# Attention with two sets of scores, keys on partitions in the second, in place of transposed probabilities

## The reference

```python
qh = (q @ Wq.T + bq).reshape(B, N_HEADS, Sq, HEAD_DIM)      # 16 heads of 16
kh = (k @ Wk.T + bk).reshape(B, N_HEADS, Skv, HEAD_DIM)
vh = (v @ Wv.T + bv).reshape(B, N_HEADS, Skv, HEAD_DIM)
scores = einsum('bhqd,bhkd->bhqk', qh, kh) / sqrt(HEAD_DIM)
scores = where(causal, -inf, scores)
out = einsum('bhqk,bhkd->bhqd', softmax(scores), vh)
x = x + out.reshape(B, Sq, E) @ Wp.T + bp
x = x + lowprec(gelu(lowprec(layernorm(x), w_fc) + b_fc), w_proj) + b_proj
```

## Time and profile before

| | |
|---|---|
| median of 3 runs | 271.9 us (270.83 to 273.41) |
| span of the profiled execution | 269.2 us |
| attention stage, first mask to the first `ffn_up` | 21.7 to 192.2 us |
| PE busy | 229.3 us |
| DVE busy | 200.8 us |
| ACT busy | 174.9 us |
| POOL busy | 112.7 us |
| mean granted TensorE clock | 0.962 |

### The profile page before, as it was taken

One profiled execution on the slowest core, in us unless ns is written; L12 is line 12 of the kernel. 1 busy time (PEld: TensorE's weight loads), 2 busy tenths in 40 slices (PEclk: granted clock), 3 DMA queues, 4 the chain that ended last, 5 costly groups with the idle time before them and its releaser, 6 DMA issues.

```text
span 269.2 us, 6301 instructions
## 1 busy us (share of the span) xinstructions
PE 229.3 (85%) x2256; PEld 172.3 (64%) x2264; DVE 200.8 (75%) x439; ACT 174.9 (65%) x463; POOL 112.7 (42%) x113
## 2 busy tenths in 40 slices
PE   7877992998999999999999999889749579789963
PEld 7765762776677777777777877667427356456752
DVE  4432473678678979979979776787798999999970
ACT  1344672567967867876876876798835646478962
POOL 2700011003524624633642641441716474569893
PEclk9997997799999999999999999999998979799999
DMA  6681694044334234224225115213031000001111
GB/s 202 170 253 41 198 262 91 2 83 86 69 75 95 71 73 94 72 64 87 49 53 105 43 44 98 61 26 55 2 49 29 19 23 19 33 29 39 42 58 58
DMA packets 37662, 20.35 MB, mean 76 GB/s; under 512 B 12788, under 2 KB 37376, under 8 KB 37632
## 3 DMA queue, kind: packets, MB, share of 16 engines
q1 hardware_dynamic: 34560, 17.14, 27.5%
q10 hardware_dynamic: 3072, 2.82, 3.5%
HBM read 7.35 MB, written 2.10 MB: 35 GB/s over the span
## 4 chain that ended last, share of the span: by engine, by line
PE 48%; DVE 27%; issue 8%; SPq 6%; DMA 5%; POOL 2%; ACT 2%; ACTq 1%; DVEq 0%; POOLq 0%
PE bank L953 13%; PE bank L1015 8%; PE s_banks L1003 7%; DVE hrn L905 7%; DVE h_amax L888 6%; PE s_banks L997 5%; DVE probT L733 5%; PE bank L1057 5%; PE bank L1038 4%; DMA QS<-full 3%; DMA w_rows<-in_L_xattn_Wq 2%; SPq L249 2%; PE bank L929 2%; SPq L242 2%; POOL hq L628 1%
## 5 line engine op out<-in xcount | busy, mean ns | idle before, releaser
L392 ACT ACTIVATE prob<-s_banks,negm 128x128 f32<-128x128 f32 x256 | 72.9, 368 | 38.3 <-DVE negm L725 36.7
L725 DVE TENSOR_REDUCE negm<-s_banks 128x4 f32<-128x512 f32 x64 | 43.8, 686 | 29.4 <-PE s_banks L1003 29.1
L733 DVE COPY probT<-bank 128x512 f32<-128x512 f32 x64 | 43.9, 687 | 10.4 <-PE bank L1015 10.4
L1015 PE MATMUL bank<-ident_f,prob 128*128 128x128 f32 x256 | 41.5, 286 | 7.9 <-DVE probT L733 7.9
L628 POOL TENSOR_TENSOR hq<-hrn,h_mag 128x1024 bf16<-128x1024 f32 x16 | 30.6, 1912 | 24.5 <-DVE hrn L905 24.2
L1015 PEld LDWEIGHTS bank<-ident_f,prob 128*128 128x128 f32 x256 | 28.0, 143 | 16.2 <-issue 12.6
L953 PE MATMUL bank<-cT,wT 128*128 128x256 f32 x128 | 33.2, 406 | 0.0
L525 POOL TENSOR_TENSOR rs<-ve,neg_half 128x2 f32<-128x2 f32 x8 | 6.3, 790 | 56.3 <-DVE ve L678 56.0
L997 PE MATMUL s_banks<-mask_q,ident_b 128*128 128x256 bf16 x128 | 19.9, 280 | 10.0 <-POOL QC L553 5.1
L478 ACT ACTIVATE s_banks<-s_banks 128x512 f32<-128x512 f32 x32 | 18.0, 581 | 15.2 <-PE s_banks L1164 14.6
L953 PEld LDWEIGHTS bank<-cT,wT 128*128 128x128 f32 x128 | 25.1, 206 | 3.2
(11 more groups left out here) (114 smaller groups left out, 409.3 us busy)
## 6 DMA issues: line engine op xcount, KB each, us to landing
oden<-oT SPq DMA_DIRECT2D x64, 64.0 KB, 2.4
KS<-full SPq DMA_DIRECT2D x32, 64.0 KB, 2.3
VS<-full SPq DMA_DIRECT2D x64, 32.0 KB, 2.0
out<-full SPq DMA_DIRECT2D x16, 128.0 KB, 1.7
QS<-full SPq DMA_DIRECT2D x29, 64.0 KB, 2.3
X<-in_x ACTq DMA_DIRECT2D x1, 1536.0 KB, 7.7
cbuf<-in_ctx SPq DMA_DIRECT2D x6, 256.0 KB, 3.0
fc_rows<-in_L_ffn_w_fc SPq DMA_DIRECT2D x1, 1024.0 KB, 5.9
```

Of the source, the lines that this page charges most:

```text
L392: ins = nc.scalar.activation(prob[:, k % 4, u, s, :], s_banks[:, 2 * (k % 2) + u, s * P:(s + 1) * P], ACT.Exp, bias=negm[:, k % 4, u, s:s ...
L725: V.tensor_reduce(negm[:, k % 4, :, :], s_banks[:, 2 * (k % 2):2 * (k % 2) + 2, 0:2 * P].rearrange("p u (s t) -> p u s t", s=2), axis=AX.X ...
L733: V.tensor_copy(probT[:, k % 4, :, :, :].rearrange("p u s t -> p (u s t)"), pt_bank(k)[:, :])\
L1015: ins = T.transpose(pt_bank(k)[:, (2 * u + s) * P:(2 * u + s + 1) * P], prob[:, k % 4, u, s, :], ident_f[:, :])
```

## The change

The scores are computed twice. The first set is as before, queries on partitions, and serves only for the maxima. `turn_maxima` transposes these for two segments at once (16 rows of 128 on TensorE), `copy_maxima` copies them to `negmT` on VectorE, and `move_maxima` moves them by DMA, one for each segment, into row 16 of each group of QC. `keys_apart`, new on ScalarE, copies KS to KX, in which row 16 is 1. The second set has keys on partitions and queries along the columns, with 17 rows: the product then holds score minus maximum. Its exponentials need no bias and are already what `attend` needs, so `transpose_probs`, `copy_pt` and `probT` go. `exps` is two instructions of 128x512.

A `burst` computes both sets: the first for segment s, the second for segment s - 3. Both lie in one bank for each group, with one mask matmul of 512 columns over all four blocks. The mask tile grows from 2 to 4 blocks. Within a burst's banks VectorE and ScalarE take turns: `exps` starts at banks 2 and 3 while `maxes` reads 0 and 1, then they change. The end of the attention stage is written out by hand with bursts that hold one set or both. SyncE's order in a step changes, with the two `move_maxima` in it. QC and KX have three buffers. On GpSimd `power2` stands ahead of `normalise`.

```diff
+NS = NW * NPAIR
...
+LAST = NS - NW
+BURSTS = [(s, s - 3 if s > 2 else None) for s in range(LAST)] + \
+    [(LAST, 25), (None, 26), (29, 27), (30, None), (None, 28), (31, 29), (None, 30), (None, 31)]
+BURST_S = {a: n for n, (a, t) in enumerate(BURSTS) if a is not None}
+BURST_T = {t: n for n, (a, t) in enumerate(BURSTS) if t is not None}
+S_BEFORE = [sum(a is not None for a, t in BURSTS[:n]) for n in range(len(BURSTS) + 1)]
+T_BEFORE = [sum(t is not None for a, t in BURSTS[:n]) for n in range(len(BURSTS) + 1)]
+UNITS = [(2 * u, 2 * u + 1) for u in range(NS // 2 - 1)] + [(30,), (31,)]
...
-        mask_q = sb("mask_q", [P, 2, P], bf16)
+        mask_qt = sb("mask_qt", [P, 4, P], bf16)
...
-        QC = [sb(f"QC{n}", [P, 2 * NM, P]) for n in range(2)]
+        KX = [sb(f"KX{n}", [P, 2 * NM, P]) for n in range(3)]
+        QC = [sb(f"QC{n}", [P, 2 * NM, P]) for n in range(3)]
...
+            def move_maxima(u):
+                sp.wait_ge(sm["mt_copied"], u + 1)
+                for h, s in enumerate(UNITS[u]):
+                    i, w = divmod(s, NW)
+                    sp.dma_start(QC[i % 3][HD::32, 2 * w:2 * w + 2, :].rearrange("p n t -> p (n t)"),
+                                 negmT[u % 2][8 * h:8 * h + 8, :])\
+                      .then_inc(sm["m_moved" if u < len(UNITS) - 1 else "ml_moved"], 16)
...
+                if not first:
+                    move_maxima(2 * i - 1)
                 if not last:
-                    if not first:
-                        sp.wait_ge(sm["s_done"], NW * i)
                     stack_rows(i + 1, 1 - par, 0)
-                if not first:
-                    move_out(i - 1)
-                if not last:
                     if not first:
                         sp.wait_ge(sm["q_apart"], i)
                     stack_rows(i + 1, 1 - par, 1)
+                move_maxima(2 * i)
+                if not last:
                     if not first:
                         sp.wait_ge(sm["v_done"], i)
                     stack_values(i + 1, 1 - par)
+                if not first:
+                    move_out(i - 1)
                 if i < NPAIR - 4:
                     load_ctx(i + 2, par)
             for i in range(NPAIR):
                 step(i, i % 2, i == 0, i == NPAIR - 1)
+            move_maxima(15)
+            move_maxima(16)
             move_out(NPAIR - 1)
...
-            def exps(k):
...
+            def exps(t):
+                n = BURST_T[t]
+                act.wait_ge(sm["burst_done"], n + 1)
+                if t > 1:
+                    act.wait_ge(sm["av_done"], t - 1)
+                for h in (1, 0):
+                    if h == 0 and BURSTS[n][0] is not None:
+                        act.wait_ge(sm["max_done"], 2 * S_BEFORE[n] + 1)
+                    nc.scalar.activation(prob[:, (2 * t + h) % 4, :, :, :].rearrange("p u s t -> p u (s t)"),
+                                         s_banks[:, 2 * h:2 * h + 2, 2 * P:4 * P], ACT.Exp)\
+                        .then_inc(sm["exp_done"], 1)
+            def keys_apart(p, par):
+                act.wait_ge(sm["k_stacked"], 16 * NG * (p + 1))
+                if p > 2:
+                    act.wait_ge(sm["burst_done"], BURST_T[NW * (p - 2) - 1] + 1)
+                nc.scalar.copy(KX[p % 3][:, :, :].rearrange("p n (j w) -> p n j w", j=NJ // KC),
+                               KS[par][:, :].rearrange("p (j n w) -> p n j w", j=NJ // KC, n=2 * NM))\
+                    .then_inc(sm["k_apart"], 1)
...
             def step(i, par, first, last):
-                k = 2 * NW * i
+                if last:
+                    return
+                k = NW * i
+                if k > 2:
+                    exps(k - 3)
+                copy_tx(i + 1)
+                copy_proj(i + 1, 0)
+                if i > 1:
+                    invert(i - 2)
+                if k > 2:
+                    exps(k - 2)
+                    copy_out(i - 1, 0)
+                copy_v(i, par)
+                copy_proj(i + 1, 1)
+                if k > 2:
+                    exps(k - 1)
+                copy_proj(i + 1, 2)
                 exps(k)
-                exps(k + 1)
...
                 if not first:
                     copy_out(i - 1, 1)
-
...
                 if ahead(i):
                     copy_tc(i + 2)
-                if not first and not last:
...
+                keys_apart(i + 1, 1 - par)
+            keys_apart(0, 0)
             steps(act, step)
+            exps(25)
+            copy_weights(0)
+            exps(26)
+            copy_weights(1)
+            invert(NPAIR - 3)
+            exps(27)
+            copy_out(NPAIR - 2, 0)
+            copy_v(NPAIR - 1, 1)
+            copy_weights(2)
+            copy_weights(3)
+            exps(28)
+            copy_out(NPAIR - 2, 1)
+            exps(29)
+            copy_tq(0, 0)
+            copy_tq(1, 1)
+            exps(30)
+            copy_out(NPAIR - 1, 0)
+            invert(NPAIR - 2)
+            exps(31)
...
-            def maxes(k):
...
+            def maxes(s):
+                n = BURST_S[s]
+                dve.wait_ge(sm["burst_done"], n + 1)
+                if s > 3:
+                    dve.wait_ge(sm["mt_done"], UNIT_OF[s - 4] + 1)
+                for h in range(2):
+                    if h and BURSTS[n][1] is not None:
+                        dve.wait_ge(sm["exp_done"], 2 * T_BEFORE[n] + 1)
+                    V.tensor_reduce(negm[:, s % NW, 2 * h:2 * h + 2, :],
+                                    s_banks[:, 2 * h:2 * h + 2, 0:2 * P].rearrange("p u (s t) -> p u s t", s=2),
+                                    axis=AX.X, op=ALU.max, negate=True).then_inc(sm["max_done"], 1)
+            def copy_maxima(u):
+                dve.wait_ge(sm["mt_done"], u + 1)
+                if u > 1:
+                    dve.wait_ge(sm["m_moved"], 16 * (UNITS[u - 2][-1] + 1))
+                n = 2 * len(UNITS[u]) * NG
+                V.tensor_copy(negmT[u % 2][0:n, :], t_bank[0:n, 0:P]).then_inc(sm["mt_copied"], 1)
...
+            def burst(n):
+                s, t = BURSTS[n]
+                if s is not None and s % NW == 0:
+                    pe.wait_ge(sm["k_apart"], s // NW + 1)
+                    pe.wait_ge(sm["q_apart"], s // NW + 1)
+                if n:
+                    pe.wait_ge(sm["max_done"], 2 * S_BEFORE[n])
+                    pe.wait_ge(sm["exp_done"], 2 * T_BEFORE[n])
+                if t is not None:
+                    if t < NS - 1:
+                        pe.wait_ge(sm["m_moved"], 16 * (UNITS[UNIT_OF[t]][-1] + 1))
+                    else:
+                        pe.wait_ge(sm["ml_moved"], 16)
+                lo, hi = (0 if s is not None else 2), (4 if t is not None else 2)
                 for g in range(NG):
-                    T.matmul(s_banks[:, g, 0:2 * P], ident_b[:, :], mask_q[:, :, :].rearrange("p s t -> p (s t)"),
...
+                    T.matmul(s_banks[:, g, lo * P:hi * P], ident_b[:, :],
+                             mask_qt[:, lo:hi, :].rearrange("p s t -> p (s t)"), start=True, stop=False)
+                for c, of in enumerate((s, t)):
+                    if of is None:
+                        continue
+                    i, w = divmod(of, NW)
+                    for h in range(2):
+                        for g in range(NG):
+                            rows = slice(32 * g, 32 * g + HD + c)
+                            queries = QC[i % 3][rows, 2 * w + h, :]
+                            keys = KX[i % 3][rows, 2 * w + h, :]
+                            ins = T.matmul(s_banks[:, g, (2 * c + h) * P:(2 * c + h + 1) * P],
+                                           *((keys, queries) if c else (queries, keys)),
+                                           start=False, stop=(h == 1 and (c == 1 or t is None)))
+                ins.then_inc(sm["burst_done"], 1)
+            def turn_maxima(u):
+                pe.wait_ge(sm["max_done"], 2 * UNITS[u][-1] + 2)
+                if u:
+                    pe.wait_ge(sm["mt_copied"], u)
+                n = 2 * len(UNITS[u]) * NG
+                w = UNITS[u][0] % NW
+                T.transpose(t_bank[0:n, 0:P],
+                            negm[:, w:w + len(UNITS[u]), :, :].rearrange("p w g n -> p (w g n)"), ident_f[:, :])\
+                    .then_inc(sm["mt_done"], 1)
...
-            def attend(i, w):
-                pe.wait_ge(sm["pt_copied"], 2 * (NW * i + w) + 2)
+            def attend(t):
+                i, w = divmod(t, NW)
+                pe.wait_ge(sm["exp_done"], 2 * t + 2)
                 if w == 0:
                     pe.wait_ge(sm["v_copied"], i + 1)
-                if w % 2 == 0 and (w or i):
-                    pe.wait_ge(sm["o_copied"], 2 * i + w // 2)
+                if w % 2 == 0 and t:
+                    pe.wait_ge(sm["o_copied"], t // 2)
                 for s in range(2):
                     b, m = divmod(2 * w + s, NM)
                     for g in range(NG):
```

(92 more changed lines are left out.)

148 lines of the change are left out of this document (32 added, 116 removed).

## The result

The median is 331.6 us (329.05 to 336.22, 4 runs) beside 271.4 (269.80 to 273.41) for the kernel before on the same chip, a ratio of 1.218 with a 95% interval of 1.208 to 1.227. That lies inside the range of 303 to 336 and 10.6 above the 321 predicted. The profiled execution has a span of 334.4, against 269.2 before. It lies near the upper end of its runs, so some 5 of the 65 us by which the spans differ are that execution's own.

A forecast was written before the change was run, and what follows sets the result against it. TensorE bounds the kernel before, SyncE's queue the changed one. Start 2.6, six steps 24.7 and tail 11.8 over 269.2 give 308.3; plus 2.7 to the median, 311; plus half of 20 for the clock, 321 us, range 303 to 336.

The forecast's parts named there:

- What bounds, and the arithmetic: Attention stage: TensorE bounds the kernel before; 4.8 us added against 5.0 removed a step, so its own step becomes 20.6.
- the row: Profile row of today's 16 score passes in a burst, 0.65 us, taken as the price of the second scores.
- The mechanism: Attention steps: bursts wait for maxima queued behind other SyncE issues, 29 where 25 were; a step is 25.0 or 24.4 us.
- First stall: Ahead of burst(4i+3): TensorE waits 1.8 us for maxima issued behind Q on SyncE.
- Second stall: Ahead of the next burst(4i+1): TensorE waits 2.0 us for maxima issued behind V, move_out and ctx.
- T+11.3: Step times count from T, the start of burst(4i+1); V waits until T+11.3 for the copy of the third projection.
- The clock: TensorE after the new stalls: clock may fall to 0.50 for 3.4 us, costing 1.7 each; half of 20 us taken.
- twelve possible falls: Two stalls a step over six steps; if all lower the clock, 12 x 1.7 = 20 us, so 331.
- Start: Up to burst(5): burst(3) waits for the first maxima until 43, then runs mostly at half clock; +2.6 us.
- Tail: burst(29) to ffn_up(0): maxima and move_out in SyncE's queue make it near 27 where it was 15.3; +11.8 us.
- The 2 us given back: Between ffn_up(0) and the first h_amax: no transposes or copies left there, -2 us, cancelled by +2 for half clock.
- rival 3: Attention stage: maxima arrive in time, six steps -0.2 each, start +2.6, tail +3; 276 us, range 271 to 280; chance 0.05.

The follow-up runs named there:

- experiment 5: Changed kernel with maxima moved into scratch and no burst waiting; invert later on ScalarE, queries_apart ahead of the weights' rounding on GpSimd: 277.6 us, ratio 1.037.
- Experiment 7: Whole changed kernel with the maxima issued on ScalarE's DMA queue instead of SyncE's, and invert later: 285.2 us, ratio 1.066.
- experiment 1: Changed kernel with only SyncE's order altered, first maxima of a step issued ahead of Q, second ahead of move_out: 312.5 us, ratio 1.160.
- experiment 6: Whole changed kernel with both sets of maxima earlier in SyncE's order, invert later, and queries ahead of the rounding on GpSimd: 288.4 us, ratio 1.079.
- experiment 8: Changed kernel with SyncE's order kept, only invert later on ScalarE and queries ahead of the rounding on GpSimd: 337.2 us, ratio 1.257.
- experiment 4: Changed kernel with dummy matmuls filling TensorE's stalls, 18 ahead of burst(4i+1) and 5 ahead of burst(4i+3), waits kept: 326.8 us, ratio 1.215.
- experiment 3: Changed kernel with the maxima's transfers kept at their places but sent into scratch, no burst waiting, maximum not subtracted: 289.3 us, ratio 1.072.

## Why the prediction was right, and where it was not

**What bounds, and the arithmetic: right.** The prediction has TensorE's own step at 20.6 where it was 20.8. With both waits gone (experiment 5), the six steps hold 116.3 us of TensorE work where the kernel before has 117.1, and take 20.2 each. The second set of scores costs 0.55 (121.01 to 121.56) where the sum has 0.65 from the row, with masks 0.96 where it has 0.97; a burst is 2.06 and not 2.27. By the rule of the Trainium skill, page TensorEngine Tiling (Array Packing), section Theoretical Speedup, the passes would have taken 0.43. So the row was the nearer of the two by a little, 0.10 against 0.12.

**The mechanism: right, shown by order and by queue.** Experiment 7 moves the same transfers to another queue, experiments 1 and 6 further to the front of the same one. Either takes away most of TensorE's wait for maxima, 42.8 us in all: 10.8 are left in experiment 1, 9.1 in 6 and 7.6 in 7, and 7.7, 4.6 and 5.5 of these are the one wait of the start. Experiments 6 and 7 have invert later as well, but that alone (experiment 8) gains nothing, and the order alone (experiment 1) gains 19 us. A transfer's own 1.9 us is then hidden. The rule of the Trainium skill, page DMA: Bandwidth & Descriptors, section Rules for kernel authors (issue early, wait late), agrees with these three; in the changed kernel it doesn't help, since there the issue is early in the program and late in its queue.

**First stall: the size roughly right.** 1.8 predicted, 1.3 measured, and the difference is the landing. The prediction has it 2.3 us after the start of the second issue; it came after 1.8 (that issue started near 123.63, half-way through the two at 123.03, and TensorE went on at 125.43). The half clock is not the reason. It delays burst(4i+2), but it delays Q's copy and issues by as much, and in the first step, where the clock is 1.00 and burst(6) comes 5.06 after burst(5), the stall is 1.33 too:

```profile
57.83 1.03 PE L1049 MATMUL s_banks<-mask_qt,ident_b 128*128 128x512 bf16 x4
62.89 1.03 PE L1049 MATMUL s_banks<-mask_qt,ident_b 128*128 128x512 bf16 x4
68.85 1.02 PE L1049 MATMUL s_banks<-mask_qt,ident_b 128*128 128x512 bf16 x4 [1.33 <-DMA QC<-negmT]
```

**Second stall: 2.0 predicted, 4.2 measured in the step shown, 3.0 to 4.9 in all six.** For a step with a context load, as this one, the prediction has V issued from T+11.3, maxima landing at T+25.0 and TensorE ready at T+22.7. Measured: V from T+13.7, landed T+28.5, TensorE ready at T+24.3. The half clock at the head of the step delays Q, the copies and V by 2.4, and V's eight issues took 6.23 for 5.05. TensorE made up part of the delay, as its bursts are shorter than 2.27 and its first stall shorter than 1.8; the queue, full to the end, did not. With the clock held (experiment 4) a step is 25.1 to 25.2, 0.7 over the sum.

**The clock: the mis-sized term.** The prediction has twelve possible falls of 1.7 us and takes half, 10. There were five in the six steps, near that half in number, but each lasted longer than the 3.4 us of the row (by the mean clock of the stretches 6 to 8.5 us) and cost 2.8 to 3.9; experiment 4 gives 3.1 by another way. So it is some 16 us and not 10. The prediction put both idles at the border of the rows that it had the earlier trace rows, and the sum of the queue had an error larger than the distance from that border. The six steps' +42.5 are then 24.7 of the sum, some 16 of the clock and about 2 of error in the sum. That the measured 331.6 is nearly the prediction's 331 for all twelve falls is chance. It is made up of fewer and dearer falls, and of a start 1.8 and a tail 6.6 longer than in its sum.

**Start: +2.6 predicted, +4.4 measured.** burst(3) started at 43.2, predicted 43, but burst(5) at 57.8 and not 56. The prediction lets the half clock end with burst(3). It lasted through burst(4) and most of the project behind it, as the stretches show:

```profile
43.20:50.00 6.80, 5.35 (x42) 3.06 (x43) 2.78 (x7) 2.62 (x4) 1.04 (x1) 0.50 0.20 50
50.00:57.80 7.80, 7.80 (x64) 5.40 (x65) 3.17 (x8) 1.78 (x3) 0.00 (x0) 0.58 0.04 14
```

**Tail: +11.8 predicted, +18.4 measured.** Its waits are the ones that the prediction names, but the stretch ran at a mean clock of 0.70, for which the sum has only +2: TensorE's 26.6 us of work there are 19 where the clock holds (experiments 5 to 7). burst(34) was put near 225 to 240 and came at 247.4. That burst(34) waits 3.6 for maxima behind move_out is as predicted. The 2 us given back ahead of the first h_amax came (257.49 to 259.76, 2.3 where it was 4.65) and mostly went again. VectorE's residual of pair 6 waits 2.60 for its projection and not 1.11. The projection ran at a clock of 0.50 and took 3.8 us (266.50 to 270.34) where it took 2.4 before (203.61 to 206.00), at a clock that was back at 1.00 by its second half:

```profile
270.59 0.69 DVE L812 TENSOR_TENSOR X<-bank,X 128x512 f32<-128x512 f32 x1 [2.60 <-PE bank L1115]
```

**What was not seen: invert.** The prediction says that what is late next is "invert, normalise and move_out of the next step", and gives it no price. In the changed kernel that was right, as the longer wait covers it. But it means that rival 3 was no rival at 276: with the maxima in time (experiment 3) the kernel took 289, since invert then was the wait; 277.6 came only with invert later too (experiment 5).

## What to carry to other kernels

A transfer's delay is its place in the issuing engine's queue more than its flight: list what stands ahead of the issue, each group with its own wait, before calling it early. When a transfer is moved later (move_out behind V), look for the engine that waits for its landing and what stands behind that wait; here it was hidden by a longer wait and worth 12 us once that was gone. And where a sum gives TensorE long idles in every turn of a loop (3.0 us and more in this one), count the lower clock behind them as a term of its own, since it also delays the queue that caused the idle.

## What the runs showed of the hardware that I had not expected

TensorE's granted clock was at 0.50 after idles of 3.90 and 4.18 us, and stayed there for at least 5.75 us of unbroken work behind the first and 7.9 behind the second; the rows of before had a stay of 3.4 us. After 1.33 us of idle it did not fall. The length of an idle alone does not settle it: in experiment 1 an idle of 2.75 us (up to 161.63) was followed by work at 1.00, in the kernel before one of 1.80 by a fall. Two small SBUF-to-SBUF transfers, 8 rows each, took 1.2 us to issue, the same 0.6 each as transfers of 64 KB, and landed under 2 us after the last issue's start. V's eight issues took from 5.09 to 6.37 us in the steps of the changed kernel (5.04 to 5.75 in the kernel before). In the group of 6.23 us it is one issue that took 1.7 and not 0.6; I did not settle why.
